# Tiles of one expert's rows halved to 128, two to a job; second weights held resident; row fetches moved to ScalarE's queue; a table made in nine pieces

## What is computed

```python
h = _layernorm(x) * (1 + ca) + sa
x = x + ga * _L0_attn_ref(h, ...)          # silu MLP, trained over the sequence by a scan of 1024 steps
h = _layernorm(x) * (1 + cb) + sb
# _L0_ffn_ref(h):
vals, idx = jax.lax.top_k(softmax(h @ w_router.T), 2)
gates = sum(one_hot(idx, 8) * vals[..., None], axis=-2)
acc = gelu(h @ Ws1.T + bs1) @ Ws2.T + bs2   # the shared expert
y[e] = gelu(h @ W1[e].T + b1[e]) @ W2[e].T + b2[e]
x = x + gb * SCALE * (acc + sum over e of gates[e] * y[e])
```

## Time and profile before

| | |
|---|---|
| median of three runs | 632.59 us (632.34 to 633.63) |
| the profiled execution | 631.76 us |
| its span in the trace | 630.0 us |
| PE busy | 565.8 us (90%) |
| DVE busy | 438.0 us (70%) |
| POOL busy | 390.9 us (62%) |
| ACT busy | 332.2 us (53%) |

### The profile page before, as it was taken

How to read it: one execution, slowest core, us unless ns; L and a number is a source line. 1 busy time by engine, 2 the same in 40 slices (tenths; PEclk the granted TensorE clock), 3 DMA queues, 4 the chain that set the end, 5 groups by cost and what they waited for, 6 DMA issues and landing times. The chain is left out here.

```text
span 630.0 us, 14425 instructions
## 1 busy us (share of the span) xinstructions
PE 565.8 (90%) x4292; PEld 509.7 (81%) x4292; DVE 438.0 (70%) x1744; ACT 332.2 (53%) x1064; POOL 390.9 (62%) x598
## 2 busy tenths in 40 slices
PE   2469999999999999999997778879979999999993
PEld 2349999899998999999985467768869999999992
DVE  3736888888888788888886488984584554444567
ACT  2455666666566666666653265676334434444441
POOL 1525566666656666665662606888888887777661
PEclk9999999999999999999999678799999999999997
DMA  9069930000000000000000000126454767777956
GB/s 202 1 267 394 395 152 1 2 0 0 0 0 0 0 0 0 0 0 0 1 3 1 2 1 31 45 81 229 118 151 133 206 181 224 228 244 245 351 175 179
DMA packets 39796, 66.77 MB, mean 106 GB/s; under 512 B 7522, under 2 KB 26724, under 8 KB 39748
## 3 DMA queue, kind: packets, MB, share of 16 engines
q1 hardware_dynamic: 31220, 54.45, 27.5%
q0 software_dynamic: 4544, 9.45, 4.2%
q10 hardware_dynamic: 3984, 2.30, 1.5%
HBM read 36.26 MB, written 29.92 MB: 105 GB/s over the span
## 5 line engine op out<-in xcount | busy, mean ns | idle before, releaser
L1582 ACT ACTIVATE hid<-bank,slab 128x256 f32<-128x256 f32 x156 | 63.1, 472 | 84.9 <-PE bank L1442 69.8
L2045 POOL DMA_INDIRECT ys<-yo,dst x78 | 75.9, 973 | 36.3 <-DVE yo L1922 18.1
L2037 POOL DMA_INDIRECT xs<-hrow,slot_i x64 | 63.6, 994 | 35.8 <-issue 35.8
L1442 PE MATMUL bank<-hg,slab 128*128 128x256 f32 x312 | 74.0, 381 | 4.5 <-issue 4.1
L1456 PEld LDWEIGHTS bank<-slab,hid 128*128 128x128 f32 x624 | 75.8, 192 | 2.0
L1456 PE MATMUL bank<-slab,hid 128*128 128x128 f32 x624 | 76.0, 275 | 0.0
L1442 PEld LDWEIGHTS bank<-hg,slab 128*128 128x128 f32 x312 | 56.3, 190 | 11.5 <-issue 5.2
L1917 DVE TENSOR_TENSOR yb<-bank,slab 128x256 f32<-128x256 f32 x39 | 16.6, 425 | 64.3 <-PE bank L1456 46.4
L990 POOL TENSOR_TENSOR nL<-aL,ones 128x128 f32<-128x128 bf16 x32 | 16.9, 527 | 42.2 <-ACT aL L699 42.2
L413 PE MATMUL bank<-aH,W2p 128*128 128x128 f32 x192 | 42.4, 303 | 0.1
L413 PE MATMUL bank<-kv,W1b 128*128 128x128 f32 x192 | 41.4, 298 | 0.0
(11 more groups left out here) (349 smaller groups left out, 1873.0 us busy)
## 6 DMA issues: line engine op xcount, KB each, us to landing
slab<-in_slabs_dram SPq DMA_DIRECT2D x39, 578.0 KB
xs<-fill SPq DMA_DIRECT2D x34, 528.0 KB
xt<-xs SPq DMA_DIRECT2D x39, 132.0 KB
yg<-ys SPq DMA_DIRECT2D x7, 512.0 KB, 4.5
xr<-in_L_attn_x_dram SPq DMA_DIRECT2D x16, 128.0 KB, 6.7
ys<-yo,dst POOLq DMA_INDIRECT x78
out_dram<-xr SPq DMA_DIRECT2D x18, 64.0 KB
xs<-hrow,slot_i POOLq DMA_INDIRECT x64
```

What stands on the lines that cost most here:

```text
L1442: mm = pe.matmul(e_half(i, n), left[:, n * P:(n + 1) * P], right, start=True, stop=True)
L1582: nc.scalar.activation(hid[i % 2][:, n, :], e_half(i, n), ACT.Gelu_apprx_tanh, bias=bias).then_inc(e_x, 1)
L2037: pool.indirect_dma_start(out=xs[:, :], out_offset=bass.IndirectOffsetOnAxis(ap=slot_i[:, i, c:c + 1], axis=0), in_=hrow[:, c, :], in_offs ...
L2045: pool.indirect_dma_start(out=ys[:, :], out_offset=bass.IndirectOffsetOnAxis(ap=dst[v][:, s:s + 1], axis=0), in_=yo[v][:, s, :], in_offset ...
```

## The change

- A tile is now a pair of halves of 128 slots (`HALF`), and each half may belong to another expert. The table has an entry for each half: `N_HALVES` = 72, so `N_TILES` = 36 jobs of experts, 43 jobs in all; `N_FULL` is 12 pairs, `FULL` = 24 halves.
- The slab of a job is two parts of 128 x 644 numbers (first weights and biases, one part per half), each fetched by its own DMA of 322 KB. The ring `RW` goes from 5 to 4. The second weights of all 8 experts (`w2`, 128 x 8 x 512 numbers, 2.1 MB) are loaded once, by SP, ahead of its wait for the table.
- PE's up product takes each half's columns with its own weights: 16 passes of 128 columns. In the down product the weights are addressed through a register: PE loads the two experts' numbers ahead of it.
- ACT makes the activation in eight pieces of 128 columns, with the bias of each half. Behind `e_gelu(i)` of an expert job it issues the row fetch of tile j + 4: two index loads and two DMAs of 66 KB. SP keeps the rows of the first four tiles.
- `meta` on DVE takes one step more, since a tile has two expert numbers. The second part of the table has 48 entries (before 30) and is made in nine pieces, behind jobs 1 to 9.
- `hid` uses the buffers `hs` of the stage before.

```diff
-SLAB = 2 * F + FT + D
-N_TILES = (2 * B * S) // TS + E - 1
+SLAB = F + FT + D
+HALF = P
+N_HALVES = -(-((2 * B * S) // HALF + E - 1) // SUB) * SUB
+N_TILES = N_HALVES // SUB
...
-N_FULL = -(-(B * S - E * (TS - 1)) // TS)
+N_FULL = -(-(B * S - E * (HALF - 1)) // HALF) // SUB
+FULL = N_FULL * SUB
...
-RW = 5
+RW = 4
...
-            slab = [psb(f"slab{i}", [P, SLAB]) for i in range(RW)]
+            slab = [psb(f"slab{i}", [P, SUB, SLAB]) for i in range(RW)]
+            w2 = psb("w2", [P, E, F])
             hg = [psb(f"hg{i}", [P, TS]) for i in range(2)]
-            hid = [psb(f"hid{i}", [P, FT, TS]) for i in range(2)]
+            hid = hs
...
+            def rows(eng, j):
+                if j >= RX:
+                    eng.wait_ge(e_tx, j - RX + 1)
+                    eng.wait_ge(meta_ready, j - RX + 1)
+                for s in range(SUB):
+                    row = eng.value_load(row_i[0:1, SUB * j + s:SUB * j + s + 1], min_val=0, max_val=XS_ROWS - HALF)
+                    eng.dma_start(xt[j % RX][:, s, :], xs[bass.ds(row, HALF), :]).then_inc(s_xt[j % RX], 16)
...
                 def weights(j):
                     if j >= RW:
                         sp.wait_ge(e_yb, job["expert", j - RW] + 1)
-                    e = sp.value_load(e_i[0:1, j:j + 1], min_val=0, max_val=E - 1)
-                    sp.dma_start(slab[j % RW][:, :], slabs[:, bass.ds(e, 1), :].rearrange("p o w -> p (o w)")).then_inc(s_slab[j % RW], 16)
-
...
+                    for s in range(SUB):
+                        e = sp.value_load(e_i[0:1, SUB * j + s:SUB * j + s + 1], min_val=0, max_val=E - 1)
+                        sp.dma_start(slab[j % RW][:, s, :], slabs[:, bass.ds(e, 1), :].rearrange("p o w -> p (o w)")).then_inc(s_slab[j % RW], 16)
+
+                sp.dma_start(w2[:, :, :], e_w2).then_inc(s_w2, 16)
                 sp.wait_ge(table_ready, 2)
                 for j in range(RW):
                     weights(j)
                 sp.wait_ge(s_half[0], 16 * CH)
-                for j in range(N_FULL):
-                    rows(j)
-                    if j >= RW:
-                        weights(j)
+                for j in range(RX):
+                    rows(sp, j)
+                for j in range(RW, N_FULL):
+                    weights(j)
                 sp.wait_ge(table_ready, 4)
-                weights(N_FULL)
-                weights(N_FULL + 1)
-                sp.wait_ge(s_half[1], 16 * CH)
                 for j in range(N_FULL, N_TILES):
-                    rows(j)
-                    if j >= N_FULL + 2:
-                        weights(j)
+                    weights(j)
                     if j == LOAD_AT:
                         scattered(sp, BY_HALF)
                     if LOAD_AT <= j < LOAD_AT + 4:
...
-                        pe.wait_ge(s_slab[j % RW], 16 * (j // RW + 1))
+                        pe.wait_ge(s_slab[j % RW], 16 * SUB * (j // RW + 1))
                         pe.wait_ge(e_hg, j + 1)
...
-                        mm = pe.matmul(e_half(i, n), left[:, n * P:(n + 1) * P], right, start=True, stop=True)
+                        if kind == "expert":
+                            for s in range(SUB):
+                                mm = pe.matmul(e_half(i, n)[:, s * P:(s + 1) * P], slab[j % RW][:, s, n * P:(n + 1) * P],
+                                               hg[j % 2][:, s * P:(s + 1) * P], start=True, stop=True)
+                        else:
...
+                    if kind == "expert":
+                        if j == 0:
+                            pe.wait_ge(s_w2, 16)
+                            pe.wait_ge(table_ready, 2)
+                        if j == N_FULL:
+                            pe.wait_ge(table_ready, 4)
+                        expert = [pe.value_load(e_i[0:1, SUB * j + s:SUB * j + s + 1], min_val=0, max_val=E - 1) for s in range(SUB)]
                     if i >= 2:
                         pe.wait_ge(e_yb, i - 1)
                     for s in range(SUB):
...
-                            right = slab[j % RW][:, F + n * P:F + (n + 1) * P] if kind == "expert" else sw[:, 1, n, :]
+                            right = w2[:, bass.ds(expert[s], 1), n * P:(n + 1) * P].rearrange("p o w -> p (o w)") if kind == "expert" else sw[:, 1, n, :]
                             mm = pe.matmul(y[:, s * D:(s + 1) * D], hid[i % 2][:, n, s * P:(s + 1) * P], right,
...
-                        bias = slab[j % RW][:, 2 * F + n:2 * F + n + 1] if kind == "expert" else sb1[:, n:n + 1]
-                        nc.scalar.activation(hid[i % 2][:, n, :], e_half(i, n), ACT.Gelu_apprx_tanh, bias=bias).then_inc(e_x, 1)
+                        if kind == "expert":
+                            nc.scalar.activation(hid[i % 2][:, n, 0:P], e_half(i, n)[:, 0:P], ACT.Gelu_apprx_tanh,
+                                                 bias=slab[j % RW][:, 0, F + n:F + n + 1])
+                            nc.scalar.activation(hid[i % 2][:, n, P:TS], e_half(i, n)[:, P:TS], ACT.Gelu_apprx_tanh,
+                                                 bias=slab[j % RW][:, 1, F + n:F + n + 1]).then_inc(e_x, 1)
...
+                    kind, j = JOBS[i]
+                    if kind == "expert" and j + RX < N_TILES:
+                        if j + RX == N_FULL:
+                            act.wait_ge(table_ready, 4)
+                            act.wait_ge(s_half[1], 16 * CH)
+                        if j == 0:
+                            act.wait_ge(table_ready, 2)
+                        rows(act, j + RX)
...
+
...
-                def rest_experts():
+                def rest_seen():
                     then(dve.tensor_tensor(later, cut["tile"][:, 0:n_rest].unsqueeze(2).broadcast_to([P, n_rest, V]),
                                            last[:, :, :].rearrange("p k e -> p (k e)").unsqueeze(1).broadcast_to([P, n_rest, V]), ALU.is_ge))
+
+                def rest_experts():
                     then(dve.tensor_reduce(etab[:, rest], later, AX_X, ALU.add))
...
+                def rest_lists():
                     for k in range(1, 3):
                         then(dve.scalar_tensor_tensor(out=etab[:, rest], in0=later[:, :, k * E - 1], scalar=-float(E), in1=etab[:, rest],
                                                       op0=ALU.mult, op1=ALU.add))
                     dve.tensor_scalar(e_i[:, rest], etab[:, rest], float(E - 1), None, ALU.min).then_inc(table_ready, 1)
 
+                def rest_weights():
...
+                def rest_weights():
+                    then(dve.tensor_tensor(later, later, weight[:, :].unsqueeze(1).broadcast_to([P, n_rest, V]), ALU.mult))
+
+                def rest_first():
+                    then(dve.tensor_reduce(first[:, rest], later, AX_X, ALU.add))
+
                 def rest_rows():
-                    then(dve.tensor_tensor(later, later, weight[:, :].unsqueeze(1).broadcast_to([P, n_rest, V]), ALU.mult))
-                    then(dve.tensor_reduce(first[:, rest], later, AX_X, ALU.add))
                     then(dve.tensor_tensor(rowf[:, rest], cut["tile"][:, 0:n_rest], first[:, rest], ALU.subtract))
-                    then(dve.tensor_scalar(rowf[:, rest], rowf[:, rest], marks[:, 0:1], float(TS), ALU.add, ALU.mult))
+                    then(dve.tensor_scalar(rowf[:, rest], rowf[:, rest], marks[:, 0:1], float(HALF), ALU.add, ALU.mult))
                     then(dve.scalar_tensor_tensor(out=rowf[:, rest], in0=etab[:, rest], scalar=float(CAP), in1=rowf[:, rest],
...
-                    e = etab[:, j:j + 1]
-                    dve.scalar_tensor_tensor(out=row2[:, :], in0=xt[r][:, :, D + 1], scalar=e, in1=xt[r][:, :, D],
-                                             op0=ALU.not_equal, op1=ALU.add)
-                    dve.scalar_tensor_tensor(out=gt[v][:, :], in0=xt[r][:, :, D + 1], scalar=e, in1=xt[r][:, :, D + 3],
-                                             op0=ALU.not_equal, op1=ALU.mult).then_inc(meta_step, 1)
-                    dve.wait_ge(meta_step, j + 1)
+                    dve.tensor_tensor(other[:, :], xt[r][:, :, D + 1], etab[:, SUB * j:SUB * (j + 1)], ALU.not_equal).then_inc(meta_step, 1)
+                    dve.wait_ge(meta_step, 2 * j + 1)
+                    dve.tensor_tensor(row2[:, :], other[:, :], xt[r][:, :, D], ALU.add)
+                    dve.tensor_tensor(gt[v][:, :], other[:, :], xt[r][:, :, D + 3], ALU.mult).then_inc(meta_step, 1)
+                    dve.wait_ge(meta_step, 2 * j + 2)
...
                     elif i == 3:
+                        rest_lasts()
+                    elif i == 4:
+                        rest_seen()
+                    elif i == 5:
                         rest_experts()
-                    elif i == 4:
+                    elif i == 6:
+                        rest_lists()
+                    elif i == 7:
+                        rest_weights()
+                    elif i == 8:
+                        rest_first()
+                    elif i == 9:
                         rest_rows()
...
```

(25 more changed lines are left out.)

57 lines of the change are left out of this document (27 added, 30 removed).

## The result

The changed kernel took 636.12 us (median of 8 runs, 634.4 to 640.68) against 632.25 us (8 runs) for the kernel before: a ratio of 1.0069, 95% interval 1.0044 to 1.0094. Slower by 0.7%, where I had forecast 621.1 us and a range of 617.5 to 636.0. Most of this part is about how both can be true.

A forecast was written before the change was run, and what follows sets the result against it. The prediction took PE to bound the last stage, with holes where the table delays `hg`. Its terms, -11.2 + 1.8 - 3.4 + 1.0 + 0.3 = -11.5 us, took 632.6 to 621.1 us, range 617.5 to 636.

The forecast's parts named there:

- Fewer jobs: Last stage on PE: 36 expert jobs of two halves instead of 39, three fewer at 3.73 us, -11.2 us.
- up product in halves: PE's up product: 16 passes of 128 columns instead of 8 of 256, 36 jobs x 0.05 us, +1.8 us.
- The table in nine pieces: DVE: smaller pieces between copies of `hg` remove most of PE's 3.87 us of holes, -3.4 us, bounds -2 and -3.9.
- Registers on PE: PE's sequencer: two index loads and eight address steps a job hide behind queued matmuls, nothing; +49 us if all exposed.
- GELU and rows on ACT: ACT: eight activations of 128 columns and two row fetches a job overlap, nothing; bounds 0 and +47 us.
- Slabs late: Weight slabs with four ring buffers: DMA falls behind 0.4 us in each of four late jobs, +1.0 us, bounds 0 and 4.
- the rest: Remaining small costs: `meta` step on DVE, doubled rows in the first table, POOL's scattering, dispatch; +0.3 us.
- (a): Rival: PE's sequencer becomes the bound through register loads or addresses, up to 670 us; chance 0.08.
- (b): Rival: ACT becomes the bound if row fetches do not overlap activations, 643 us, up to 667; chance 0.07.
- (c): Rival: slabs come late, landing 0.7 us later in each of 22 jobs, +15, 636 us; chance 0.07.
- my own list of signs: Gaps ahead of down products for (a), or with ACT's activation just done for (b); gaps ahead of up products for (c).
- (d): Rival: smaller gain, table pieces still delay `hg` and the late stretch loses 3 to 4 us, 624 to 630 us; chance 0.10.

The follow-up runs named there:

- chip B: Chip of the second group of runs, with no late signal on DVE; the unedited changed kernel took 619.04 us there, ratio 0.9831.
- the first chip: Chip of the first measurement, number not on record: the changed kernel against the kernel before, 636.12 us, ratio 1.0069.
- f0_again: The changed kernel, unedited, run again on chip C against the kernel before: 636.17 us, ratio 1.0054.
- f2_before_dose: The kernel before, with four extra DVE operations (some 2.6 us) ahead of the post in six jobs, on chip C: 641.07 us, ratio 1.0121.
- d1_again: The changed kernel, unedited, run again on chip B against the kernel before: 619.04 us, ratio 0.9831.
- the first four edits: Changed kernel with PE's loads out, pieces ahead of posts, POOL runs of two, or table in four pieces: 618.73, 617.29, 621.18, 624.13 us.
- My last group: Changed kernel with four extra DVE operations ahead of the post in six jobs, on chip F: 632.42 us, ratio 1.0038.
- chip C: Chip of the third group of runs, with late signals of its own; the unedited changed kernel took 636.17 us there, ratio 1.0054.

## Why the prediction failed, point by point

*The step that failed* is a premise under several terms, the table's above all: that DVE and ACT go on as soon as PE's product ends.

*Fewer jobs, up product in halves.* Right. A product in halves takes 1.79 us against 1.73, +2.2 us for 36 jobs where I had +1.8.

*The table in nine pieces, -3.4.* This step failed in the measurement that counts. On chip B it holds: 4.6 us were lost ahead of up products before, on the first chip, and 0.5 are now. On the first chip it is 9.9: 6.2 in the three stops behind late posts and pieces, 1.8 at 516.46 behind a post 4.15 us late, 1.0 at 601.92 behind a slab, and 0.9 in small ones. The table's own stops thus went from 4.2 to 6.2 us, +2.0 where I had -3.4, and all that stands ahead of up products is +5.2. I set the pieces beside a DVE that is half free and took for granted that a post starts when its product ends. With the post 2.2 us late, post, scaling and copy take up nearly all of the 3.6 us that PE has work for, and a piece of 1.35 us is a stop.

*Registers on PE, nothing; GELU and rows on ACT, nothing.* Right where signals come in time: PE lost 0.4 us outside the stops. Where they are late, 6.2 us go there. My reading is that a late `hg` holds PE's sequencer, it starts the loads with fewer matmuls queued, and the array waits; part stands ahead of down products, where ACT's late activations are waited for. That this is how the 6 us come about is argued from the order of the rows and not shown; the kernel that leaves the loads out met only chips without late signals.

*Slabs late, +1.0.* One stop of 0.81 us at 601.92 on the first chip, two (0.56 and 1.01 us) in f0_again, none on B.

*The end.* Not in my sum: from the last expert's down product to the end it is 16.1 us before, 17.8 on the first chip, 18.0 on B. In the chain the last landing of `yg` takes 4.15 us where it took 3.56, and on the first chip the last post comes 1.1 us late; on B the landing takes 5.57. Why it is longer there stays open.

*The sum.* On B, against the trace of before on the first chip: -11.2 + 2.2 - 4.1 for the stage, +1.9 at the end, -0.6 at the start is -11.8 us, where the traces differ by 11.9; on B itself 619.04 against 630.65 us, -11.6, was measured. That my -11.5 meets this is in part luck: the end, which I had at nothing, cost 1.9 us, the slabs and "the rest", which I had at 1.3, cost nothing, and the table gave 0.7 more. On the first chip the stage loses 11.1 us more than before to waits (16.1 against 5.0), which eats the 9.0 of the jobs; with 0.4 at the start and 1.7 at the end the trace is 4.4 us longer.

*The rivals.* (a) and (b) are excluded by B. (c) is 0.8 us on the first chip and 1.6 in f0_again. By my own list of signs, gaps ahead of up products spoke for (c); the large ones here waited for `hg`. (d) had the place right, pieces that delay `hg`, but gave it 624 to 630 us and knew of no late signal. The one that decided was missing from the list: signals of PE that come late and posts with no room for it.

*Slips in the working.* 36 x 1.4 is 50, not 49. In (c) a landing 0.7 us late, less the 0.5 of slack, gives 22 x 0.2 = 4.4 us and not 15. The windows of the earlier trace rows reach from 460 to 600 us and hold some 37 jobs, not 46. The chances of (a) to (c) add to 0.22, where the last line gives slower 0.18. None of these moves the forecast.

**Two questions stay open.** The first is what holds the signals: the chip, the occasion or the recording, for every run on record has a recorded span and clock and none shows the kernel without them. In the three late traces without a dose each signal over 0.5 us late arrives while POOL issues indirect DMAs or within 1.4 us of the end of one; but such times make up about nine tenths of the stage, so that alone says little. The latest (2.4 us and more) stand behind three or more in a row. The longest is the post at 515.08 us, whose product ended at 510.93, 4.15 us earlier; POOL's last DMA ended at 514.11:

```profile
511.89 0.96 POOL L2090 DMA_INDIRECT ys<-yo,dst  x1 [0.30 <-issue]
513.15 0.96 POOL L2090 DMA_INDIRECT ys<-yo,dst  x1 [0.30 <-issue]
514.10 1.29 POOL L2065 MEMSET rested<- 128x1408 f32 x1
```

But chip B has the same runs of four and no late signal, so they are not enough by themselves, and the kernel with runs of two never met a chip where it could show anything. The second is why the changed kernel's signals are later than those of the kernel before in the same measurement (33 us in sum against 22 on DVE, the latest 4.15 us against 1.94); f2_before_dose speaks against its being only less tolerant.

## What to carry to other kernels

Before costing work into the free time of an engine, measure how late its releases are: end of the producer against start of the waiter, over the whole stage. An engine that is half busy but in-order, with a release 2 us late in a period of 3.7, has no room. And put a control, the unedited kernel, into every group of runs: here the chip or the occasion moved the ratio from 0.983 to 1.005, more than any edit, and without d1_again each of the first four edits would have looked like the cure. My last group lacks that control too.

## What the runs showed of the hardware

I had not expected chips or occasions to differ in this. On two of the seven occasions (first measurement and chip C) PE's semaphore increments reached DVE and ACT up to 2.7 us, and twice more (3.84 and 4.15 us), after the recorded end of the matmul, while PE's passes went on every 0.11 us, and SP's register steps of 18 to 150 ns took up to 719. On the other five the posts followed their products within about 0.1 us, one excepted (0.46 us), and the register steps took 18 to 154 ns. The kernel before notes it little: its medians were 632.25 and 632.99 us with late signals, and 627.6 to 632.0 on the five chips without, where the changed kernel went from 636.1 and 636.2 to 619.0. Most of its lateness falls where PE has other work.
